# Expert results added into three sums in DRAM, the first of which starts as the residual

## What is computed

```python
# x: (64, 128, 256), context: (64, 128, 192); 4 heads of 64
x1 = x + attention(x, context, mask)            # keys: context and x
n1 = layernorm(x1)                              # hidden_states of the FFN
scores = sigmoid(n1 @ router_weight.T)          # 32 experts, 4 groups of 8, the best 2 groups
topk_idx, topk_w = best 4 experts of each token, weights divided by their sum, times 2.5
hidden_vals = silu(n1 @ gate_w[e].T) * (n1 @ up_w[e].T)        # 128 wide
mixed = sum over the 4 chosen e of topk_w * (hidden_vals @ down_w[e].T)
shared = (silu(n1 @ shared_gate_w.T) * (n1 @ shared_up_w.T)) @ shared_down_w.T
out = x1 + mixed + shared
```

## Time and profile before

| | |
|---|---|
| runs | 1344.24 us median, 1341.73 to 1345.44 |
| profiled execution | 1343.46 us, its span 1341.5 us |
| mean granted TensorE clock | 0.985 of full speed |
| TensorE busy | 1298.0 us (97%) |
| ScalarE busy | 1011.6 us (75%) |
| VectorE busy | 972.0 us (72%) |
| GpSimd busy | 643.4 us (48%) |
| DMA | 247.14 MB, mean 184 GB/s |
| attention stage with its end | 0 to about 742 us |
| tile stage | about 742 to 1193 us |
| last stage | about 1193 to 1341.5 us |

### The profile page before, as it was taken

How to read it: one execution, slowest core, us unless ns; L and a number is a source line. 1 busy time by engine, 2 the same in 40 slices (tenths; PEclk the granted TensorE clock), 3 DMA queues, 4 the chain that set the end, 5 groups by cost and what they waited for, 6 DMA issues and landing times.

```text
span 1341.5 us, 32944 instructions
## 1 busy us (share of the span) xinstructions
PE 1298.0 (97%) x8718; PEld 1043.2 (78%) x8718; DVE 972.0 (72%) x4498; ACT 1011.6 (75%) x2730; POOL 643.4 (48%) x724
## 2 busy tenths in 40 slices
PE   6999999999999999999979899999999999999997
PEld 4566676676676766766658799999999999988886
DVE  4578898888988988888887455555555555548887
ACT  4899999999999999999851566766776676653332
POOL 1113555555555555555455366666666666640000
PEclk8999999999999999999989899999999999999999
DMA  8234645535545445454487655555655555438896
GB/s 278 84 133 136 205 162 176 192 131 187 176 138 190 161 153 195 136 179 162 168 304 246 194 169 172 172 172 168 178 169 174 169 173 166 132 114 313 304 319 218
DMA packets 147714, 247.14 MB, mean 184 GB/s; under 512 B 24139, under 2 KB 110413, under 8 KB 146896
## 3 DMA queue, kind: packets, MB, share of 16 engines
q1 hardware_dynamic: 121472, 177.63, 41.3%
q0 software_dynamic: 26064, 67.42, 14.5%
HBM read 104.68 MB, written 119.96 MB: 167 GB/s over the span
## 4 chain that ended last, share of the span: by engine, by line
PE 63%; ACT 21%; DVE 9%; issue 5%; DMA 2%; SPq 0%; POOL 0%; ACTq 0%; DVEq 0%
PE psT L1033 10%; PE ps L1033 9%; PE psS L1043 9%; ACT arena L1168 6%; PE ps L916 6%; PE ps L1024 5%; PE ps L852 4%; ACT arena L1160 4%; PE psS L927 3%; PE psT L827 3%; PE psS L813 3%; PE psO L840 2%; ACT arena L1128 2%; ACT arena L1132 2%; ACT arena L1175 2%
## 5 line engine op out<-in xcount | busy, mean ns | idle before, releaser
L701 POOL DMA_INDIRECT expert_out<-pay,dest x287 | 282.1, 983 | 175.1 <-DVE dest L1878 157.4
L556 POOL DMA_INDIRECT lists<-pay,slot x168 | 174.3, 1037 | 187.7 <-PE psT L827 39.6
L1043 PE MATMUL psS<-arena,history 128*128 x574 | 171.8, 381 | 0.3 <-DVE history L1865 0.3
L1033 PEld LDWEIGHTS ps<-pad,hist_j 128*128 128x128 f32 x1152 | 152.1, 193 | 9.5 <-ACT pad L1315 2.1
L1033 PEld LDWEIGHTS psT<-pad 128*128 128x128 f32 x1144 | 151.0, 192 | 7.3
L1033 PE MATMUL ps<-pad,hist_j 128*128 128x128 f32 x1152 | 152.8, 276 | 1.9 <-ACT pad L1315 1.9
L1033 PE MATMUL psT<-pad 128*128 128x128 f32 x1144 | 151.6, 276 | 0.0
L1872 DVE TENSOR_SCALAR pay<-psS,dest 128x256 f32<-128x256 f32 x287 | 138.9, 484 | 1.6 <-PE psS L1043 1.5
L757 PE MATMUL ps<-arena 128*128 128x512 f32 x256 | 128.3, 624 | 2.6 <-ACT arena L1120 2.0
L556 POOL DMA_INDIRECT lists<-arena,slot x88 | 91.0, 1034 | 79.4 <-PE psT L827 20.6
L1168 ACT ACTIVATE arena<-arena,rden 128x256 f32<-128x256 f32 x256 | 109.1, 503 | 15.2 <-DVE rden L1466 15.1
(11 more groups left out here) (238 smaller groups left out, 3284.1 us busy)
## 6 DMA issues: line engine op xcount, KB each, us to landing
lists<-pad SPq DMA_DIRECT2D x72, 516.0 KB, 5.2
pay<-lists SPq DMA_DIRECT2D x287, 129.0 KB, 2.2
arena<-expert_out SPq DMA_DIRECT2D x32, 1024.0 KB, 7.1
pay<-pay SPq DMA_DIRECT2D x42, 384.0 KB, 3.6
x<-in_x SPq DMA_DIRECT2D x32, 256.0 KB, 4.7
out<-arena SPq DMA_DIRECT2D x31, 256.0 KB, 5.8
arena<-arena SPq DMA_DIRECT2D x20, 384.0 KB, 3.4
arena<-in_ctx SPq DMA_DIRECT2D x32, 192.0 KB, 4.6
```

Source lines behind the costliest of these rows:

```text
L556: pool.indirect_dma_start(lists, bass.IndirectOffsetOnAxis(ap=slots(u)[:, j, k:k + 1], axis=0), paid(u)[:, j, k, :], None).then_inc(scat[3 ...
L701: pool.indirect_dma_start(expert_out, bass.IndirectOffsetOnAxis(ap=dest[:, t % DESTS, 1:2], axis=0), yy[n], None, bounds_check=T * TOPK - ...
L1033: m = pe.matmul(ps[2 + n % 2][:, which * P:(which + 1) * P], w_now[1 - n % 2][:, k, which * I:(which + 1) * I], xsT[:, n % 2, k * P:(k + 1 ...
L1043: pe.matmul(dbank[n % 2][:, 0:D], hh[:, n % 4, :], w_dn[:, at(e, 1), :].rearrange("p a n -> p (a n)"), start=True, stop=True)\
```

## The change

- `expert_out` and `n1T_kept` go. Three sums in DRAM (`sums`, [8192, 256] each) come. The result of tile t is added into sum t mod 3 by an indirect DMA with an add. It waits for the scatter of tile t-3, the last one into the same sum. `places` now gives the token's row, the same for its four choices.
- The first sum starts as x1: SP stores a unit's x1 when its residual is complete (`keep_x1`). The other two start as zeros (`zero_sums`, one store in each step, from `pad`). GpSimd waits for all of these before the first tile's scatter; ScalarE awaits the zeros before it writes into `pad`.
- The place of a unit in `x1` in SBUF then takes its turned rows: `n1_copy` writes them there for all 32 units, after the store of that unit has landed. So the save, the load, `mr`, `norm_again`, `shared_turn` and `turned` go; `shared_up` reads the turned rows from x1.
- The shared result is written over them: `add_shared` becomes a copy on VectorE for units 0 to 7, and `keep_shared` a copy on ScalarE for units 8 to 30. For unit 31 the last addition reads PSUM.
- The gate and up weights come in three loads after the attention's last reads (experts 0 to 7, 8 to 16, 17 to 31); TensorE and ScalarE await four loads instead of seven. The late down weights are those of ten experts instead of twelve.
- In the last stage SP loads two units of the three sums at a time, three deep (`er`), and VectorE makes a sum of three.

```diff
-    expert_out = nc.dram_tensor("expert_out", [T * TOPK, D], fp32).ap()
-    n1T_kept = nc.dram_tensor("n1T_kept", [EARLY, P, 2 * D], fp32).ap()
+    sums = [nc.dram_tensor(f"sums{n}", [T, D], fp32).ap() for n in range(SUMS)]
...
+        by_batch = [v.rearrange("(p b) n -> p b n", p=P) for v in sums]
...
+        def n1T_of(n):
+            return x1[:, 2 * n:2 * n + 2, :]
...
+            def keep_x1(u):
+                sp.wait_ge(y_done, 2 * u.n + 2)
+                ge(sp, e_n, u.n - 1)
+                sp.dma_start(by_batch[0][:, at(2 * u.n, 2), :], x1[:, at(2 * u.n, 2), :]).then_inc(x1_kept[u.par], 16)
+            def zero_sums(n):
+                a, m = n % (SUMS - 1) + 1, n // (SUMS - 1) * FILL
+                sp.dma_start(by_batch[a][:, m:m + FILL, :], pad[:, :, 0:D]).then_inc(zeroed, 16)
...
-                if s.n == UNITS - 1:
-                    load_n1T()
                 if (s + -2).exists():
                     spread_rows(s + -2)
+                if (s + -1).exists():
+                    keep_x1(s + -1)
                 if s.exists():
                     blank_unit(s)
-                if (s + -2).exists() and s.n - 2 < EARLY:
-                    save_n1T(s + -2)
+                zero_sums(s.n)
...
+            sp.wait_ge(hats, UNITS)
+            sp.wait_ge(pb_full, NB)
+            sp.wait_ge(pc_full, NB)
+            sp.wait_ge(ss_done, NB)
+            load_experts(0, below_wo // 2)
+            load_experts(below_wo // 2, below_wo)
             spread_rows(Unit(UNITS // 2 - 1, 0))
-            sp.wait_ge(y_done, NB)
+            keep_x1(Unit(UNITS // 2 - 1, 1))
             load_experts(below_wo, E)
...
             for t in range(TILES):
                 load_tile(t, t % SLOTS)
                 if t == 1:
-                    sp.wait_ge(sgu_full, 2 * EARLY)
-                    load_experts(above - 1, above)
                     sp.dma_start(w_dn[:, early:E], down[:, early:E]).then_inc(weights_l, 16)
...
+            def load_er(w):
+                ge(sp, dD, 2 * (w - ER_DEPTH + 1))
+                for a in range(SUMS):
+                    sp.dma_start(er[:, w % ER_DEPTH, a], by_batch[a][:, at(4 * w, 4), :]).then_inc(er_in[w % ER_DEPTH], 16)
...
+                ge(pool, y_out[(t - SUMS) % SLOTS], 16 * ((t - SUMS) // SLOTS + 1))
                 pool.indirect_dma_start(
-                    expert_out, bass.IndirectOffsetOnAxis(ap=dest[:, t % DESTS, 1:2], axis=0),
-                    yy[n], None, bounds_check=T * TOPK - 1, oob_is_err=False).then_inc(y_out[n], 16)
+                    sums[t % SUMS], bass.IndirectOffsetOnAxis(ap=dest[:, t % DESTS, 1:2], axis=0),
+                    yy[n], None, bounds_check=T - 1, oob_is_err=False, compute_op=ALU.add).then_inc(y_out[n], 16)
...
             def n1_copy(u):
                 act.wait_ge(t_n, u.n + 1)
                 ge(act, lg_full, u.n)
-                ge(act, n1T_saved, 16 * upto(u.n, EARLY))
-                act.activation(n1T.rearrange("p k n -> p (k n)"), n1_bank(u)[:, :], ACT.Copy).then_inc(e_n, 1)
+                act.wait_ge(x1_kept[u.par], 16 * (u.i + 1))
+                act.activation(n1T_of(u.n).rearrange("p k n -> p (k n)"), n1_bank(u)[:, :], ACT.Copy).then_inc(e_n, 1)
...
             for u in range(EARLY, UNITS):
-                if u + 1 < UNITS:
-                    norm_again(u + 1)
                 shared_silu(u, 0)
-                if u + 1 < UNITS:
-                    turned(u + 1)
                 shared_silu(u, 1)
+                if u > EARLY:
+                    keep_shared(u - 1, 0)
+                    keep_shared(u - 1, 1)
...
             def sum_experts(v):
-                dve.wait_ge(er_in[v % ER_DEPTH], 16 * (v // ER_DEPTH + 1))
-                four = er[:, v % ER_DEPTH]
-                dve.tensor_tensor(e2, four[:, :, 0:2, :], four[:, :, 2:4, :], ALU.add).then_inc(dC, 1)
+                if v % 2 == 0:
+                    dve.wait_ge(er_in[v // 2 % ER_DEPTH], 16 * SUMS * (v // 2 // ER_DEPTH + 1))
+                parts = er[:, v // 2 % ER_DEPTH, :, v % 2 * 2:v % 2 * 2 + 2, :]
+                ge(dve, dD, v)
+                dve.tensor_tensor(e2, parts[:, 0], parts[:, 1], ALU.add).then_inc(dC, 1)
+                ge(dve, res_done, v)
                 dve.wait_ge(dC, v + 1)
-                dve.tensor_tensor(esum, e2[:, :, 0, :], e2[:, :, 1, :], ALU.add).then_inc(dD, 1)
+                dve.tensor_tensor(esum, e2, parts[:, 2], ALU.add).then_inc(dD, 1)
```

More of the change, by code:

```diff
@@ L146, in build @@
         pay_mid = part(2, TOPK, ROW)
-        late = 2 * E + 2 * 2 * P + 2 * TOPK * E + 2 * TOPK * ROW
+        late = 2 * E + 2 * TOPK * E + 2 * TOPK * ROW
         assert used[0] <= E * 3 * D - late, (used[0], E * 3 * D - late)
@@ L248, in build @@
         rows_ready, row_copies = sem("rows_ready"), sem("row_copies")
-        n1T_saved, n1T_in = sem("n1T_saved"), [sem(f"n1T_in{n}") for n in range(EARLY)]
+        x1_kept, zeroed = [sem("x1_kept0"), sem("x1_kept1")], sem("zeroed")
         scat = [sem("scat0"), sem("scat1"), sem("scat2"), sem("scat_last")]
@@ L339, in rsqrt @@
             link(nc.vector.scalar_tensor_tensor(y, t, 9.0 / 16.0, g, ALU.add, ALU.mult))
+        by_batch = [v.rearrange("(p b) n -> p b n", p=P) for v in sums]
         def wide(v):
             return v.rearrange("(a n) -> a n", a=1).to_broadcast([P, v.shape[0]])
-        er = arena[:, 0:ER_DEPTH * 2 * TOPK * D].rearrange("p (a j k n) -> p a j k n", a=ER_DEPTH, j=2, k=TOPK)
-        used[0] = ER_DEPTH * 2 * TOPK * D
-        esum, e2 = part(2, D), part(2, 2, D)
+        er = arena[:, 0:ER_DEPTH * SUMS * 4 * D].rearrange("p (w a j n) -> p w a j n", w=ER_DEPTH, a=SUMS, j=4)
+        used[0] = ER_DEPTH * SUMS * 4 * D
+        esum, e2 = part(2, D), part(2, D)
         res = part(2, 2, D)
-        late_set = [part(2 * D) for _ in range(4)]
-        first_n1T, above, below_wo = 6, 6 + EARLY, 17
-        early_n1T = arena[:, first_n1T * 2 * D:above * 2 * D].rearrange("p (u n) -> p u n", u=EARLY)
+        late_set = [part(2 * D) for _ in range(2)]
+        below_wo = 17
         up_banks = [[ps[0], ps[2]], [ps[3], ps[1]]]
[L354 to L359, removed]
+        def n1T_of(n):
+            return x1[:, 2 * n:2 * n + 2, :]
         def gated(u):
-            flat = flat_p[:, u % 2 * 2 * D:(u % 2 + 1) * 2 * D] if u < EARLY else late_set[2 + u % 2]
+            flat = flat_p[:, u % 2 * 2 * D:(u % 2 + 1) * 2 * D] if u < EARLY else late_set[u % 2]
             return flat.rearrange("p (m n) -> p m n", m=2)
@@ L488, in store @@
                 sp.dma_start(out_d[:, at(2 * v, 2), :], res[:, v % 2]).then_inc(stored[v % 2], 16)
-            for v in range(ER_DEPTH):
-                load_er(v)
+            for w in range(ER_DEPTH):
+                load_er(w)
             for v in range(UNITS - 1):
-                if v + ER_DEPTH < UNITS:
-                    load_er(v + ER_DEPTH)
+                if v % 2 == 1 and v // 2 + ER_DEPTH < UNITS // 2:
+                    load_er(v // 2 + ER_DEPTH)
                 store(v)
             for j in range(2):
-                sp.wait_ge(res_done, UNITS + j)
+                sp.wait_ge(last_done, j + 1)
                 sp.dma_start(out_d[:, 2 * UNITS - 2 + j, :], res[:, 1, j, :]).then_inc(stored[1], 16)
@@ L552, in places @@
                                    place[:, :, :].rearrange("p j (k o) -> p j k o", o=1),
-                                   float(u.n * 2 * P * TOPK), None, ALU.add).then_inc(placed, 1)
+                                   float(2 * u.n), None, ALU.add).then_inc(placed, 1)
             def scatter_row(u, j, k):
@@ L888, in _ @@
             dbank = [psS[:, 0].rearrange("p a n -> p (a n)"), psS[:, 1].rearrange("p a n -> p (a n)")]
-            def shared_turn(u):
-                pe.wait_ge(nh, u - EARLY + 1)
-                ge(pe, nt_ev, u - EARLY)
-                for j in range(2):
-                    for k in range(2):
-                        m = pe.transpose(psO[:, k * D + j * P:k * D + (j + 1) * P],
-                                         n1_of(u)[:, j, k * P:(k + 1) * P], ident[:, :])
-                m.then_inc(nt_full, 1)
             def shared_up(u, mm):
@@ L1265, in _ @@
             in_order(step, UNITS)
-            def norm_again(u):
-                ge(act, nt_full, u - EARLY)
-                for j in range(2):
-                    b = 2 * u + j
-                    a = act.activation(n1_of(u)[:, j, :], x1[:, b, :], ACT.Identity,
-                                       bias=mr[:, b, 0:1], scale=mr[:, b, 1:2])
-                a.then_inc(nh, 1)
-            def turned(u):
-                act.wait_ge(nt_full, u - EARLY + 1)
-                ge(act, sgu_full, 2 * u)
-                act.activation(n1T_of(u).rearrange("p k n -> p (k n)"), psO[:, :], ACT.Copy).then_inc(nt_ev, 1)
             def shared_silu(u, mm):
@@ L1753, in add_shared @@
                     dve.wait_ge(sd_full, 2 * u + j + 1)
[L1754 to L1755 removed]
```

(1 more changed line is left out.)

94 lines of the change are left out of this document (35 added, 59 removed).

## The result

The changed kernel takes 1434.9 us in the median of four runs (1432.4 to 1438.8) beside 1343.0 us for the kernel before (1341.2 to 1345.4): a ratio of 1.069, 95% interval 1.065 to 1.072. The forecast was 1328 with a range of 1316 to 1395: a gain of 16 us was expected, and 92 us were lost.

The account below looks back on a forecast made before the run. TensorE was taken to bound all three stages, with gaps only at their seams. Terms 0 - 2 - 2 + 0 - 12.3 = -16.3 on 1343.46 us gave 1327.2, median 1328; range 1316 to 1395, reaching into the slower rivals.

Parts of the forecast that it names:

- Attention stage: Units of attention: added x1 and zero stores fit into the emptier DMA part; 0 us, bounds -1 and +10.
- End of attention: Seam near 672 us: dropping the loads of kept turned rows removes a late scatter; -2 us, bounds -6 and +3.
- Start of the tile stage: First tiles: the wait for gate and up weights goes and tile 2 lands earlier; -2 us, bounds -4 and 0.
- Tile stage: 287 tiles: scatters become adds at an unchanged 1.541 us a tile, if landing and issue stay within bounds; 0 us.
- Condition two: Tile stage, GpSimd: an add's issue, 0.98 us for a copy, must stay below 1.24 us to not set the pace.
- rival B: Tile stage: an add's issue sets the pace from 1.24 us; +66 us at one and a half times, +206 at twice; chance 0.13.
- Condition one: Tile stage: from an add's start to its landing less than 4.62 us, three steps; 4.4 expected if read precedes write.
- DMA share: Tile stage: scatters at twice their 23.9% of the stage's 0.59 give a share of 0.83, still under 1.
- Last stage: Shared expert of units 8 to 31, sums and output: fewer turns, earlier start, later first sums, shorter tail; -12.3 us.
- turns: Last stage, TensorE: four turns removed per unit, period 5.60 to about 5.17 us; -9.5 us over 22 periods.
- the wait for the first sums: Last stage: the first sum needs 1.5 MB behind the last add, delaying VectorE; +3.7 and slow matmuls +1.3, together +5.0 us.
- The tail: End of the last stage: VectorE loses the shared result's add, but stores queue behind loads; -1.5 us, bounds -5 and +2.

Follow-up runs that it names:

- a_copy_weights: The changed kernel with plain writes instead of adds, and the loads of expert 0 to 16 weights behind unit 30's rows and the last x1 store: 1322.3 us.
- a_weights: The changed kernel with the loads of expert 0 to 16 weights moved behind unit 30's rows and the last x1 store: 1430.2 us.
- a_copy: The changed kernel with plain indirect writes into the three sums instead of adds, every wait kept: 1329.7 us, ratio 0.989 to the kernel before.
- a_third8: The changed kernel with adds for every third tile, plain copies otherwise, targets over eight arrays, no wait for the scatter three tiles back: 1329.5 us.
- b_split: The kernel before with the reloads of the turned rows of units 1 to 7 moved behind unit 29's rows: 1343.8 us beside 1344.1, ratio 0.999.
- b_seams: b_split with expert 13's gate and up weights ahead of the first tile's rows and late down weights behind tile 3: 1343.3 us beside 1344.1.
- a_third: The changed kernel with adds only for the first sum's tiles and plain copies into the other two, wait for three tiles back kept: 1361.8 us.

## Why the prediction was wrong, point by point

**Attention stage: 0.** Right. From the first to the last operation of one ScalarE line it took 642.2 us before (L1128, 17.5 to 659.7) and 642.8 after (L1111, 20.2 to 663.0): +0.6 in 31 units. It only starts later, by 2.7 us, and that is chance of the run: in the kernels with the same start as after, this first operation stands at 17.6 (`a_copy_weights`), 18.7 (`a_weights`), 20.0 (`a_copy`) and 20.1 (`a_third8`), with 642.2 to 642.5 us behind it each time, and in those with the start of before at 18.4 (`b_split`) and 19.6 (`b_seams`).

**End of attention: -2.** Wrong in sign, though inside its bound of +3: from the last of these ScalarE operations to the last `shared_down` before the tiles it took 78.3 us before (to 738.00) and 80.5 after (to 743.51), +2.2, and +1.6 in `a_copy`. The text named the place (4.3 MB of weights ahead of unit 30's rows) and priced a late landing at 6.5 us; it took 10.6, and TensorE waited 5.36 us. In `a_weights` it comes at 749.8, of which 1.5 us are its earlier start: the move of the weights is worth the other 7.8 in the traces, and 4.7 by the medians.

**Start of the tile stage: -2.** Right in sign, half the size. From that `shared_down` to the first scatter it took 16.5 us before and 15.6 after: -1.0 (-1.1 in `a_copy`). TensorE's wait for the weights (3.00 us) went, but tile 2 landed after 6.44 us and not 4.8. The chain and the timeline of the kernel after:

```profile
747.46 6.44 DMA pay<-lists
...
753.95 0.44 PE L1009 MATMUL ps<-ident,pay 128*128 128x128 f32 x2 [3.55 <-DMA pay<-lists]
```

With the late start (+2.7), +0.6, +2.2 and -1.0, the first scatter came 4.5 us later instead of 4 earlier.

**Tile stage: 0 while two conditions hold.** This is the step that failed; both conditions are broken. Condition two took the issue as a copy's 0.98 us "only" because the bound of 1.24 was well above it, though no row showed an add. It takes 1.56, and this alone is 93 of the 105.5 us. With that in rival B's own formula, (1.56 + 0.30 - 1.54) x 286 = +91, on 1328: 1419; the chain adds 9 to 13 more, and the median is 1434.9. The rule of the Trainium skill ("GPSIMD Engine Reference", section 4) that set this rival up, with one core of GpSimd for the read and another for the write descriptors, does not by itself say what an add's issue costs. The runs show 1.6 times that of a copy, mostly as a fixed part; that the second read is the reason, no run shows. Condition one (landing below 4.62 us) was met in the median, 3.9 us from 800 to 840, with 4.4 forecast from a copy and a load. But it left out the 0.84 us from a landing to the next add, so the true bound was 3.78 us, and the forecast's own 4.4 broke it: (4.4 + 0.84)/3 = 1.75 us a tile would have been +59 us.

**DMA share: 0.83.** The near match is luck. Measured 0.85, but at a pace 24% slower, since an add takes 2.5 to 2.8 times a copy. In that window a tile took 160/85 = 1.88 us; scaled to 1.541 it would be 0.85 x 1.88/1.541 = 1.04. By this estimate, which no run tests, the adds of all tiles would not have fitted into the stage even with the issue and the chain solved.

**Last stage: -12.3.** Right in kind, low by 2.6 us in the kernel after (-14.9) and 3.6 in `a_copy` (-15.9). By `a_copy`: turns -9.2 (22 periods of 5.18; forecast -9.5); start -6.5 (first `shared_down` 4.7 us after the last scatter instead of 11.2; forecast -6.3); the wait for the first sums +4.0, as 2.08 of gap and slow matmuls (118.0 us from the first to the last of the 22 periods less 113.96; forecast +5.0). The tail is the term that was mis-sized: -4.2 (7.7 us from unit 30's `shared_down` to the end instead of 11.9; forecast -1.5). The last two units' down projections now run together, with no wait of TensorE for VectorE's addition between them: 3.62 us for both instead of 5.53, which is 1.9 of the 4.2. The rest lies in what follows them and was not taken apart. In the kernel after TensorE had begun this stage's matmuls at 1290.82, while GpSimd was still behind, and then stood 15.34 us before 1318.41. That head start won nothing: from the last scatter to the end it takes 131.4 us there and 130.4 in `a_copy`.

**Chances.** Rival B had 0.13 and was argued away with the size of the copy. A quantity that no row shows, with a bound only 27% above its nearest relative, deserved more than that.

## What to carry to other kernels

An adding scatter has other costs than a plain one: measure its issue, its landing and its time on the DMA engines before it goes into every step of a loop. Ask of the engine that issues it how much it may grow before it sets the pace (here 0.26 us), and of every wait that orders adds into one target how long the landing is at the loop's load, with the time from the landing to the next issue (here 0.84 us). A third of the tiles could have been adds at no cost in time if they did not wait for each other; whether the sums are then right, no run here shows.

## What the runs showed of the hardware

- An indirect DMA of 128 rows takes GpSimd 0.984 us as a write and 1.56 us as an add; 64 rows 0.907 and 1.419; half the width changes nothing (1.552).
- The landing of an add, from its start, took 2.7 to 7.1 us in the kernel after, 4.0 in the median (3.9 from 800 to 840 us, at a DMA share of 0.85).
- An add takes 16.6 us of DMA engine time for 129 KB, a write 5.9 to 6.7. The queue shows 3044 packets for 22 adds and 1248 for 26 writes.
- A copy next to adds is a little slower to issue: 1.03 us in `a_third8`, where two of three scatters are copies.
- A GpSimd operation of 0.25 us between scatters leaves gaps of 0.17 us, and the scatter then takes 1.05 us, so it costs 0.22 us of a tile and not 0.25.
- Between the landing of a scatter and the start of a GpSimd scatter that waits for it lie 0.84 us at the least (`a_third`; 0.83 in the kernel after).
